# Two-layer kernel: the second layer's norm in half chunks, PSUM copies ahead of its roots, rotary tables loaded earlier

## The reference, cut to what matters

```
x  = x0
xn = (x - mean) / sqrt(var + 1e-5)
x  = x + recurrent_memory(xn) + expert_ffn(xn)        # layer 0
xn = (x - mean) / sqrt(var + 1e-5)                    # the norm that is changed
q, k, v = xn @ wq, xn @ wk, xn @ wv
q, k = rotary(q), rotary(k)    # first 64 of 128 columns: turn * cos + swap * sin
p  = softmax(causal(q @ k.T / 128))
x  = x + (p @ v) @ wo + gated_ffn(xn)                 # ffn with 128 -> 512 -> 512 -> 512 -> 128
```

## Time and profile before

| what | value |
|---|---|
| median of 3 runs | 276.53 us (276.32 to 276.6) |
| the profiled execution's own time | 277.21 us |
| its span, first to last instruction | 275.1 us |
| busy: PE / DVE / ACT / POOL | 258.8 / 216.1 / 191.4 / 100.8 us |
| chain that ended last | PE 58%, DVE 29%, ACT 7% |

### The profile page before, as it was taken

How to read it: one execution, slowest core, us unless ns; L and a number is a source line. 1 busy time by engine, 2 the same in 40 slices (tenths; PEclk the granted TensorE clock), 3 DMA queues, 4 the chain that set the end, 5 groups by cost and what they waited for, 6 DMA issues and landing times.

```text
span 275.1 us, 5406 instructions
## 1 busy us (share of the span) xinstructions
PE 258.8 (94%) x1794; PEld 169.7 (62%) x1798; DVE 216.1 (79%) x733; ACT 191.4 (70%) x467; POOL 100.8 (37%) x130
## 2 busy tenths in 40 slices
PE   6899999999978889999999999999999999999993
PEld 2379845456653634767777777778687444444483
DVE  6977579999997589889999979778850797666684
ACT  1487489886655379688755799999661897777730
POOL 9314000000000067898875579889772000000000
PEclk9999999999999799999999999999999999999999
DMA  7700000000000191400000000000000000000005
GB/s 198 212 14 2 2 0 4 0 1 0 2 2 0 23 397 44 152 2 4 0 2 0 0 2 0 4 1 0 0 2 2 0 0 0 4 1 0 0 10 147
DMA packets 8287, 8.51 MB, mean 31 GB/s; under 512 B 1729, under 2 KB 7362, under 8 KB 7746
## 3 DMA queue, kind: packets, MB, share of 16 engines
q1 hardware_dynamic: 7826, 7.84, 9.0%
q10 hardware_dynamic: 432, 0.30, 0.4%
HBM read 7.09 MB, written 1.05 MB: 30 GB/s over the span
## 4 chain that ended last, share of the span: by engine, by line
PE 58%; DVE 29%; ACT 7%; issue 3%; DMA 2%; SPq 0%; DVEq 0%; ACTq 0%
PE PS L862 10%; PE PS L861 10%; PE PS L834 9%; PE PS L811 8%; PE PS L824 4%; PE PS L495 3%; DVE arena L1592 3%; PE PS L514 3%; DVE arena L1579 2%; DVE arena L1624 2%; DVE arena L1829 2%; DVE mxb L1844 2%; DVE arena L1615 2%; DMA x<-L_attn_x 2%; PE PS L784 2%
## 5 line engine op out<-in xcount | busy, mean ns | idle before, releaser
L861 PE MATMUL PS<-arena 128*128 128x512 f16 x128 | 48.5, 379 | 0.0
L862 PE MATMUL PS<-arena 128*128 128x512 f16 x128 | 48.5, 379 | 0.0
L1902 DVE TENSOR_TENSOR arena<-arena 128x512 f32<-128x512 f32 x32 | 22.2, 693 | 13.6 <-ACT arena L1292 13.6
L811 PE MATMUL PS<-arena 128*128 128x512 f32 (+3 forms) x80 | 31.9, 530 | 0.0
L1291 ACT ACTIVATE arena<-PS,arena 128x512 f32<-128x512 f32 x32 | 22.7, 710 | 9.6 <-PE PS L862 9.6
L1352 POOL CAST arena<-arena 128x512 f16<-128x512 f32 x2 | 1.3, 645 | 73.6 <-ACT x L1157 73.6
L1344 POOL TENSOR_TENSOR arena<-arena 128x256 f32<-128x256 f32 x32 | 21.5, 672 | 14.5 <-DVE arena L1836 12.6
L1265 ACT ACTIVATE arena<-PS,lnt 128x512 f32<-128x512 f32 (+3 forms) x40 | 24.9, 632 | 1.6 <-DVE lnt L1851 1.4
L1345 POOL TENSOR_TENSOR arena<-arena,small 128x256 f16<-128x256 f32 (+1 forms) x36 | 23.8, 660 | 2.8
L1292 ACT ACTIVATE arena<-PS,arena 128x512 f16<-128x512 f32 x32 | 22.6, 707 | 0.0
L1844 DVE TENSOR_REDUCE mxb<-PS 128x1 f32<-128x512 f32 (+3 forms) x40 | 22.2, 602 | 0.3 <-PE PS L813 0.2
(11 more groups left out here) (282 smaller groups left out, 649.8 us busy)
## 6 DMA issues: line engine op xcount, KB each, us to landing
arena<-h_T SPq DMA_DIRECT2D x2, 1024.0 KB, 5.7
x<-L_attn_x SPq DMA_DIRECT2D x4, 256.0 KB, 4.7
arena<-cos SPq DMA_DIRECT2D x1, 1024.0 KB, 4.8
arena<-sin SPq DMA_DIRECT2D x1, 1024.0 KB, 7.0
out<-arena SPq DMA_DIRECT2D x4, 256.0 KB, 2.3
arena<-w_T SPq DMA_DIRECT2D x3, 256.0 KB, 3.0
con<-shape_constants ACTq DMA_DIRECT2D x1, 192.0 KB, 3.4
w1e<-L_ffn_W SPq DMA_DIRECT2D x1, 128.0 KB
```

What stands on the lines that cost most here:

```text
L811: i = mm(PS[:, k, 0:cnt * P], qT1[:, t * P:(t + 1) * P], kT1[:, c * P:(c + cnt) * P], start=True, stop=not last)
L861: mm(bank(b), wH[:, k, m * P:(m + 1) * P], sH[:, k, cols], start=(k == 0), stop=False)
L862: i = mm(bank(b), wL[:, k, m * P:(m + 1) * P], sL[:, k, cols], start=False, stop=(k == HT4 - 1))
L1902: v.tensor_tensor(RP[m], FP[m], high, ALU.subtract).then_inc(rest_ready, 1)
```

## The change

- **Copies first.** ScalarE copies blocks 1, 2, 3, then takes the root of block 0, and then copies block 0. All normalizing instructions now wait for the fourth copy.
- **Half chunks on VectorE.** The statistics of the next block are split: two tiles stand ahead of the inverse, one between inverse and shift, and one after the normalizing. The first rotary product of block 0 stands between the statistics of block 3 and its inverse, the other rotary work of blocks 0 and 1 comes next, and the five small scale instructions stand behind it.
- **ScalarE's order.** The transposed copies of blocks 1 and 2 stand ahead of the normalizing of blocks 2 and 3. Of block 0, ScalarE now normalizes one tile and VectorE three.
- **Tables.** Cosines and sines lie in the room of first-layer buffers (`VC`, `O1` to `O4`, `TA` to `TC`) and are loaded during the lane chain, after its 13th far product (`fp_ready` at 13, the 13th of L1680). `h1` is now loaded together with `h2`, after the last rotary addition.

```diff
-            sp.wait_ge(x1_ready, 2)
+            sp.wait_ge(fp_ready, FAR)
             for i, n in enumerate(("cos", "sin")):
                 sp.dma_start((cosT, sinT)[i], a[n]).then_inc(tab_in, 16)
-            sp.wait_ge(x1_ready, 4)
-            sp.dma_start(h1S, a["h1_T"]).then_inc(h_in[0], 16)
             sp.wait_ge(turned_dve, 4)
             sp.wait_ge(turned_pool, 4)
+            sp.dma_start(h1S, a["h1_T"]).then_inc(h_in[0], 16)
             sp.dma_start(h2S, a["h2_T"]).then_inc(h_in[1], 16)
...
@@ TensorE, normed(c) @@
-                pe.wait_ge(xn2_act, 2 * c + 2)
-                pe.wait_ge(xn2_dve, 2 * c + 2)
+                pe.wait_ge(xn2_act, 2 * c + 1)
+                pe.wait_ge(xn2_dve, 2 * c + 3)
...
@@ ScalarE @@
             def normed(c):
-                act.wait_ge(x1_ready, max(c + 1, 2))
+                act.wait_ge(x1_ready, 4)
                 act.wait_ge(shift_ready, c + 1)
-                for n in range(4 * c, 4 * c + 2):
+                for n in range(4 * c, 4 * c + (2 if c else 1)):
...
-            first_block(1)
+            for b in (1, 2, 3):
+                first_block(b)
             deviations(0)
             first_block(0)
             normed(0)
-            first_block(2)
             deviations(1)
             transposed(0)
-            first_block(3)
             normed(1)
             deviations(2)
+            transposed(1)
             normed(2)
-            transposed(1)
             deviations(3)
+            transposed(2)
             normed(3)
-            transposed(2)
...
@@ VectorE @@
             def normed(c):
-                dve.wait_ge(x1_ready, max(c + 1, 2))
-                for n in range(4 * c + 2, 4 * c + 4):
+                dve.wait_ge(x1_ready, 4)
+                for n in range(4 * c + (2 if c else 1), 4 * c + 4):
...
-            first_variances()
-            for c in range(4):
-                shifts(c)
-                normed(c)
-                if c < 3:
-                    statistics(c + 1)
-                    variances(c + 1)
+            statistics(0, 1, 2, 3)
+            variances(0)
+            statistics(4, 5)
+            i = inverse(0)
+            statistics(6)
+            shifts(0, i)
+            normed(0)
+            statistics(7)
+            variances(1)
...
+            statistics(15)
+            variances(3)
+            dve.wait_ge(tab_in, 32)
+            rope(0, 0)
+            i = inverse(3)
+            shifts(3, i)
+            normed(3)
+            rope(0, 1)
+            rope(1, 0)
+            rope(1, 1)
```

More of the change, by code:

```diff
@@ L128, in program @@
         s1, s2, sh1, sh2, s1h, s12 = (take(HT4) for _ in range(6))
-        a_tab = at[0]
         HT = take(2 * T).rearrange("p (h t) -> p h t", h=2)
-        cosT, sinT = arena[:, a_tab:a_tab + T], arena[:, a_tab + T:a_tab + 2 * T]
         a_blocks = at[0]
@@ L158, in program @@
         STf = take(SCAN * RW)
+        tab_at = at[0]
         VC = take(HALF * L).rearrange("p (j t) -> p j t", j=HALF)
         O1, O2, O3, O4, TA, TB, TC = (take(HALF * L).rearrange("p (j t) -> p j t", j=HALF) for _ in range(7))
+        assert at[0] - tab_at == 2 * T
+        cosT, sinT = arena[:, tab_at:tab_at + T], arena[:, tab_at + T:tab_at + 2 * T]
         Yf = take(L * L)
@@ L1754, in _, with statistics @@
             general_path(dve, general)
[L1756 to L1767, removed]
+            def statistics(*tiles):
+                for n in tiles:
+                    if n < 4:
+                        dve.wait_ge(ao_done, 1)
+                        did(v.bn_stats(st[:, n, :], PS[:, 0, n * D:(n + 1) * D]))
+                    else:
+                        dve.wait_ge(x1_ready, n // 4)
+                        did(v.bn_stats(st[:, n, :], x[:, n, :]))
             def variances(c):
@@ L1773, in variances, with inverse, shifts @@
                     (i.then_inc(var2_ready, 1) if n == 4 * c + 3 else did(i))
-            def shifts(c):
+            def inverse(c):
                 piece = slice(4 * c, 4 * c + 4)
                 dve.wait_ge(sd2_ready, c + 1)
-                need(did(v.reciprocal(lnt[:, 1, piece], lnt[:, 1, piece])))
+                return did(v.reciprocal(lnt[:, 1, piece], lnt[:, 1, piece]))
+            def shifts(c, after):
+                piece = slice(4 * c, 4 * c + 4)
+                need(after)
@@ L1787, in _, with rope @@
-            for c in range(4):
-                shifts(c)
-                normed(c)
-                if c < 3:
-                    statistics(c + 1)
-                    variances(c + 1)
+            def rope(c, part):
+                b = 4 * ((c + 1) % 2)
+                cols = slice(c * BANK, (c + 1) * BANK)
+                if part == 0:
+                    if c >= 2:
+                        dve.wait_ge(turned_pool, c - 1)
+                        dve.wait_ge(turned_dve, c - 1)
+                    dve.wait_ge(turn_done, 2 * c + 1)
+                    v.tensor_tensor(TURN[c % 2][:, 0, :], bank(b + 2), cosT[:, cols], ALU.mult).then_inc(rope_dve, 1)
+                else:
+                    dve.wait_ge(turn_done, 2 * c + 2)
+                    v.tensor_tensor(TURN[c % 2][:, 1, :], bank(b + 3), sinT[:, cols], ALU.mult).then_inc(rope_dve, 1)
+                    dve.wait_ge(rope_dve, 2 * c + 2)
+                    v.tensor_tensor(qT1[ROT:P, cols], TURN[c % 2][0:ROT, 0, :], TURN[c % 2][0:ROT, 1, :], ALU.add).then_inc(turned_dve, 1)
@@ new lines, in _ @@
+            statistics(0, 1, 2, 3)
[7 more added lines that the diff above has]
+            variances(1)
+            statistics(8, 9)
+            i = inverse(1)
+            statistics(10)
+            shifts(1, i)
+            normed(1)
+            statistics(11)
+            variances(2)
+            statistics(12, 13)
+            i = inverse(2)
+            statistics(14)
@@ L1794, in _ @@
+            shifts(2, i)
+            normed(2)
+            statistics(15)
[8 more added lines that the diff above has]
+            rope(1, 1)
             dve.wait_ge(small_in, 16 * 13)
@@ L1796, in _ @@
             v.scalar_tensor_tensor(out=s12, in0=s1, scalar=0.5, in1=s2, op0=ALU.mult, op1=ALU.mult).then_inc(scales_ready, 1)
-            need(did(v.tensor_tensor(s12a, s1, s2, ALU.mult)))
+            i = did(v.tensor_tensor(s12a, s1, s2, ALU.mult))
+            v.tensor_reduce(sums[:, 1:2], sh1, AX.X, ALU.add, apply_absolute_value=True).then_inc(sums_ready, 1)
+            need(i)
             v.tensor_reduce(sums[:, 0:1], s12a, AX.X, ALU.add, apply_absolute_value=True).then_inc(sums_ready, 1)
[L1799 to L1813, removed]
+            for c in (2, 3):
+                for part in range(2):
+                    rope(c, part)
             def values(c):
```

## The result

| | before | changed |
|---|---|---|
| median of 20 runs each | 277.16 us (276.3 to 280.19) | 279.47 us (276.63 to 281.84) |
| ratio, with its 95% interval | 1 | 1.0059 (1.0035 to 1.0084) |
| profiled execution: own time, span | 277.21, 275.1 us | 278.35, 276.2 us |

The change made the kernel slower, by more than forecast, and the median lies outside the range. (The three first runs of before had a median of 276.53; over 20 it is 277.16.) The ratio leaves out the executions more than 1.5% above the fastest of their kernel; of the changed kernel these are the four from 281.29 us up, which belong to its last group all the same. What stands out is the spread: the executions of the changed kernel come in groups, and a group goes with its mean granted clock.

What follows compares the result with a forecast made beforehand. It took the stage before attention to be bound by ScalarE's skip copy and first exponential, with TensorE 0.1 us behind; +0.92 -0.31 +0.51 -0.10 -0.11 gave +0.91, so 276.53 + 0.9 = 277.4 us, range 276.0 to 278.3.

Steps and rivals of the forecast that it cites:

- The first block starts later: Start of the norm: block copies ahead of the first root and three VectorE tiles delay TensorE's first transpose, +0.92 us.
- three end at 95.70 + 0.52 + 0.34: Block 0's normalizing: VectorE's three tiles start at 95.70 and end at 96.56, from the earlier pitch of two tiles.
- The transposed copy gets a third back: Block 0's transposed copy: less statistics work left on VectorE after normalizing, so part of the delay is regained, -0.31 us.
- ScalarE's new order delays block 2: Block 2's normalizing queues behind block 1's transposed copy, so TensorE's transposes of block 2 come later, +0.51 us.
- Turn 3 no longer waits: TensorE's rotary stage: ScalarE's copies come only about 0.1 later, so turn 3 need not wait, -0.10 us.
- ScalarE's slack of 0.11: Last skip copy: ScalarE had been 0.14 behind TensorE and is now 0.03 behind, -0.11 us.
- Tables and weights at 0: Lane chain and `h1` loading: early tables and the later `h1` cost and gain nothing, 0; tables' upper bound 0.7 us.
- Small scale instructions at 0: VectorE's rotary stage: reordering the small scale instructions costs nothing because VectorE is not the last, 0.
- Rival 4: TensorE's turn and swap 0 run at half clock and double, +2.7 us in all, 279.2 us; chance 0.05.
- Rival 1: VectorE paces the norm and rotary stage, so the change is faster, -0.53 us, 276.0 us; chance 0.17.

Runs made afterwards that it cites:

- e2: Changed kernel, but GpSimd's four gate-weight conversions wait until VectorE has normalized block 1; 277.37 us in like clock against 278.32.
- e3: Changed kernel with ScalarE again normalizing blocks 2 and 3 ahead of the transposed copies of blocks 1 and 2; median 279.73 us.
- e4: Kernel before with only the transfers changed: tables loaded in the lane chain, `h1` together with `h2`; ratio 1.0000.
- e6: Kernel before without six filler products around the branch ending the first layer; eight low-clock executions had median 279.2 us, the other two 277.9.
- e7: Changed kernel keeping half chunks and early tables; ScalarE's order and block 0's split as before, small scale instructions after the last normalizing; 276.21 us, ratio 0.9962.
- e1: Changed kernel with nine more filler products on TensorE, before and after the norm's first transpose; median 278.4 us, ratio 1.0055.

## Why the prediction was wrong, point by point

The direction was right, and so was the place; the size of the sum and the weight of a rival were not. Of the 2.1 us between the forecast of 277.4 and the measured 279.47, 0.6 are the base: the forecast was added to the median of three runs, 276.53, and over 20 runs it is 277.16. Some 0.3 are terms of the sum (points 1 to 4), and the rest is the low clock (point 7).

1. **"The first block starts later", +0.92.** Right as an order, short as a size. Counted from the end of the memory output (93.91 before, 93.62 now), the first transpose is 1.65 later. The copies gave what was forecast; the missing term is 0.61, the difference between 0.86 and 1.47 for three tiles, the rest of some 0.1 is handovers. The step that failed in the sum is "three end at 95.70 + 0.52 + 0.34": the tiles' pitch was taken from a stretch in which GpSimd was idle, while the edit itself moves GpSimd's conversions beside them, because they wait for the fourth copy. The prediction gave no line to that waiter. With e2 it is shown: 0.86 and -0.64.
2. **"The transposed copy gets a third back", -0.31.** Measured -0.40: 97.76 against 96.80, +1.25 in the same count.
3. **"ScalarE's new order delays block 2", +0.51.** Measured +0.53 (+1.78 at the transposes of block 2), with TensorE idle for 0.59 before them. e3 shows its cause.
4. **"Turn 3 no longer waits", -0.10.** Mis-sized: -0.42 from there to the last skip product, since all of TensorE's small waits for copies and transposes went, not only one. ScalarE's slack of 0.11 came as forecast (-0.10). At the exponential this leaves +1.27 against the forecast 0.91, and in like clock the runs show +1.18.
5. **Tables and weights at 0.** Right (e4).
6. **Small scale instructions at 0.** Right for the time, wrong as a row: the first of them stands for 1.12 us behind GpSimd's addition. VectorE was not the last, so it cost nothing.
7. **Rival 4, "the clock falls once more", 0.05.** This is where the range broke. It was priced well, +1.8 (measured +1.58 for turn and swap 0 in e3), but a group that fits it is 10 of 20 executions. Where their clock fell is argued from e3 and e6, since the one trace of the changed kernel is not of this group. The prediction gave it 0.05 because the clock had not fallen after the gap of before, which it called similar. That was one trace, and the gap grew from 0.39 to 1.88 us (the idle time ahead of the first transpose); its own sum already made it 0.92 longer. That rule of the Trainium skill, page "TensorE: Matmul & The Clock Gate", section "HAM oscillation", should have had more weight: e3 and e6 agree with it at 0.50, after idle times of 1.24 and 1.41 us ahead of the first transpose (shorter than the waits in the page's case), while the changed kernel's own profile, with 1.88, does not. Even the forecast with it, 279.2, would have been near the measured median.

The Trainium skill had a rule for point 1 too. Its page "SBUF — State Buffer", section "Who interferes with whom", says that a VectorE instruction such as tensor_scalar in its two-port mode and a GpSimd instruction take one port pair in turns, each for its whole length. The trace agrees in the main: 1.12 us for an instruction that takes 0.16 in the kernel before, and a tile set of 1.47 that falls to 0.86 when the conversions are moved. It does not agree on the whole length: the third tile ends at 96.90, in the middle of a GpSimd instruction that runs from 96.22 to 97.71. That the ports are the cause is the page's word; the runs show that the time at which the conversions run is.

The idea of half chunks was judged too low as well. Rival 1 gave -0.53 for VectorE alone and held it for hidden, as TensorE fills the stage. It was hidden only by ScalarE's edits: with these undone (e7) it brings 0.65 us by the medians and 1.05 by the ratio of 0.9962.

What stays open: how often the clock falls in a given kernel. The executions show it as a share (10 of 20, 2 of 12, 0 of 12), and no run here was made to find what decides between two executions of one kernel. The idle time ahead of the first transpose does not decide it alone: in one profile of each it is 1.88 in the changed kernel (10 of 20), 1.41 in e6 (8 of 10), 1.24 in e3 (5 of 6), 1.20 in e2 (2 of 12) and 1.12 in e7 (0 of 11).

## What to carry to other kernels

When an edit brings a semaphore forward, list all who wait for it: here the fourth block copy also let GpSimd loose on VectorE's most critical tiles. Copies and transposed copies belong behind the work that the next stage waits for, even where their own input is ready first, and independent small work belongs into the waits for a root. A longer gap on TensorE is to be priced as a chance of half clock in the next stretch, and one profile at full clock is no evidence against it: look at the clocks of many executions.

## What the runs showed of the hardware that was not expected

- One kernel has several times. The changed kernel took 276.6 to 277.0 at a mean clock of 0.995 to 0.996 and 280.3 and more at 0.975 to 0.980, with the same instructions.
- The memory output takes 2.06 us at full clock (e1, e7) and 3.41 to 3.79 at the lower one (the other profiles). Executions of the kernel before with mean clock 0.983 lie at 277.3 to 277.7, 1.0 above those at 0.996. That this stretch is the difference is likely and not shown, since the only trace of before is at 0.992.
- VectorE against GpSimd: a 128 x 4 instruction stood for 1.12 us beside a GpSimd addition, and one normalized tile of 0.34 us for 0.63 to 0.71 beside a conversion.
